# A six-step attention stage with all turns written out, and normalised rows split on ScalarE and GpSimd and transposed by DMA

## What is computed

```python
x = x + 0.5 * ffn(layernorm(x), norm_weight, router_w, router_b, fc1_w, fc1_b, fc2_w, fc2_b)
x = x + attn(layernorm(x), W_q, W_k, W_v, W_o)
x = x + 0.5 * ffn(layernorm(x), ...)

def attn(x, W_q, W_k, W_v, W_o):          # per batch: 512 rows of 256
    q, k, v = x @ W_q.T, x @ W_k.T, x @ W_v.T
    att = softmax(causal(q @ k.T / 16))
    return (att @ v) @ W_o.T

def ffn(x, ...):                          # 8 experts, each takes the 2048 rows of 16384 it rates highest
    xn = x * rsqrt(mean(x * x) + eps) * norm_weight
    probs = softmax(xn @ router_w.T + router_b)
    gates, idx = top_k(probs.T, 2048)
    ye = gelu(xn[idx] @ fc1.T + b1) @ fc2.T + b2
    return scatter_add(idx, ye * gates) / scatter_add(idx, gates)
```

## Time and profile before

| | us |
|---|---|
| median of 3 runs | 2383.83 (2383.52 to 2384.28) |
| profiled execution | 2383.67 |
| its span in the trace | 2382.0 |
| attention stage in the trace, first load to last logits | 977.1 to 1534.3 |

### The profile page before, as it was taken

One profiled execution on the slowest core, in us unless ns is written; L12 is line 12 of the kernel. 1 busy time (PEld: TensorE's weight loads), 2 busy tenths in 40 slices (PEclk: granted clock), 3 DMA queues, 4 the chain that ended last, 5 costly groups with the idle time before them and its releaser, 6 DMA issues.

```text
span 2382.0 us, 44303 instructions
## 1 busy us (share of the span) xinstructions
PE 2006.6 (84%) x15482; PEld 1428.6 (60%) x15482; DVE 1443.8 (61%) x3808; ACT 1402.4 (59%) x2776; POOL 1238.6 (52%) x1527
## 2 busy tenths in 40 slices
PE   4721599999999999499999999511899999999997
PEld 4620266666666667377777777400566666666665
DVE  6988654454454532289888888687644445445431
ACT  6911466666666665266767777401666666666663
POOL 6700566666666663243343443102666676666663
PEclk8655699999999999799999999755999999999998
DMA  8890355564566543232332332200555556456542
GB/s 279 280 312 32 105 103 90 100 118 82 92 116 98 86 74 49 54 99 83 103 105 80 106 99 77 100 1 10 138 95 107 94 100 114 83 94 118 79 68 32
DMA packets 308678, 241.30 MB, mean 101 GB/s; under 512 B 159793, under 2 KB 295985, under 8 KB 308273
## 3 DMA queue, kind: packets, MB, share of 16 engines
q1 hardware_dynamic: 251184, 172.06, 25.9%
q0 software_dynamic: 57344, 67.29, 19.4%
HBM read 120.76 MB, written 101.71 MB: 93 GB/s over the span
## 4 chain that ended last, share of the span: by engine, by line
PE 78%; DVE 12%; ACT 3%; issue 3%; POOL 2%; DMA 2%; SPq 0%; POOLq 0%; DVEq 0%; ACTq 0%
PE ps L1117 24%; PE ps L1119 24%; PE ps L1118 24%; DVE junk L866 5%; PE ps L1138 2%; PE ps L1219 1%; PE ps L1272 1%; ACT zz L612 1%; DVE nmax L1069 1%; DVE bst L793 1%; PE ps L1184 1%; PE ps L1232 1%; DMA z_d<-zz 1%; DVE seen L950 0%; POOL nt L479 0%
## 5 line engine op out<-in xcount | busy, mean ns | idle before, releaser
L978 DVE SCALAR_TENSOR_TENSOR hid_l<-hf,hid_h 128x512 f16<-128x512 f32 x512 | 355.1, 694 | 616.9 <-ACT hid_h L586 603.6
L1117 PE MATMUL ps<-w_h,hid_h 128*128 128x256 f16 x2048 | 558.2, 273 | 0.0
L1118 PE MATMUL ps<-w_l,hid_h 128*128 128x256 f16 x2048 | 558.2, 273 | 0.0
L1119 PE MATMUL ps<-w_h,hid_l 128*128 128x256 f16 x2048 | 558.2, 273 | 0.0
L661 ACT ACTIVATE hf<-ps,b 128x512 f32<-128x512 f32 x512 | 349.0, 682 | 133.2 <-PE ps L1119 121.5
L1117 PE MATMUL ps<-xt,w_h 128*128 128x512 f16 x1024 | 389.7, 381 | 33.9 <-DMA xt<-xs 33.9
L1118 PE MATMUL ps<-xt,w_h 128*128 128x512 f16 x1024 | 389.6, 380 | 0.0
L1119 PE MATMUL ps<-xt,w_l 128*128 128x512 f16 x1024 | 389.6, 380 | 0.0
L586 ACT ACTIVATE hid_h<-hf 128x512 f16<-128x512 f32 x512 | 322.4, 630 | 16.3
L586 ACT ACTIVATE ys<-ps,weight 128x256 f32<-128x256 f32 x256 | 121.5, 474 | 342.7 <-PE ps L1119 342.7
L521 POOL DMA_INDIRECT xe<-z_d,tok x256 | 261.5, 1022 | 100.3 <-issue 77.4
(11 more groups left out here) (225 smaller groups left out, 4016.5 us busy)
## 6 DMA issues: line engine op xcount, KB each, us to landing
w_st<-fc_t SPq DMA_DIRECT2D x32, 1024.0 KB, 5.4
xin<-x SPq DMA_DIRECT2D x32, 512.0 KB, 5.4
z_d<-zz SPq DMA_DIRECT2D x32, 512.0 KB, 4.1
xin<-x_d SPq DMA_DIRECT2D x32, 512.0 KB, 5.3
out<-x SPq DMA_DIRECT2D x32, 512.0 KB, 3.0
z_d<-z SPq DMA_DIRECT2D x32, 512.0 KB, 4.5
xe<-z_d,tok POOLq DMA_INDIRECT x256
xt<-xs SPq DMA_TRANSPOSE x256
```

The source lines that it names most:

```text
L978: dve.scalar_tensor_tensor(hid_l[:, n % 2, f, :], hf[:, f % HF, :], HS, hid_h[:, n % 2, f, :], ALU.mult, ALU.subtract).then_inc(s_hl, 1)
L1117: pe.matmul(dst, lh, rh, start=first, stop=False)
L1118: pe.matmul(dst, lh, rl, start=False, stop=False)
L1119: return pe.matmul(dst, ll, rh, start=False, stop=last)
```

## The change

The attention stage gets one step more. A turn c now does: the load of group c+2; statistics and row factors of group c; the zz rows of z = c-1; u and v of f = c-2; scores to residual of a = c-3; the second normalisation of r = c-4; logits of l = c-5. All 37 turns are written out, without a loop.

The sixteen f32 transposes per turn on TensorE and their PSUM halves zt_h, zt_l, z2t_h, z2t_l are gone. Instead ScalarE copies the normalised rows to f16 (zr, z2r, high half), GpSimd subtracts that from the f32 rows (low half), and SyncE issues four transposing DMAs per group and kind: zr to zc (three buffers) and z2r to z2c (one buffer). u is made in two parts that TensorE's order places apart, and VectorE makes the low half of v at the start of the next turn. xin has eight buffers in this stage, mv, zs and zb four places instead of two.

```diff
+        zr = sb("zr", [P, TG, 2, D], F16, att)
+        zc = sb("zc", [P, 3, 2, KD, S], F16, att)
+        z2r = sb("z2r", [P, TG, 2, D], F16, att)
+        z2c = sb("z2c", [P, 2, KD, S], F16, att)
...
@@ SyncE @@
+            def x_in(c):
+                wait(sp, s_x2, TG * (c - WIDE + 1))
+                sp.dma_start(xin[:, c % WIDE], group(x1_d, c)).then_inc(s_in[c % WIDE], 16)
+            def columns(dst, src, done):
+                for t in range(TG):
+                    sp.dma_start_transpose(dst[:, :, :, t * P:(t + 1) * P].rearrange("p h k s -> p (h k) s"),
+                                           src[:, t].rearrange("p h d -> p (h d)")).then_inc(done, 16)
+            def att_turn(c):
+                z, r = c - 1, c - 4
+                if on(c + 2):
+                    x_in(c + 2)
+                if on(z):
+                    sp.wait_ge(s_zrl, z + 1)
+                    wait(sp, s_s, TG * (z - 2))
+                    columns(zc[:, z % 3], zr, s_zc)
+                if on(r):
+                    sp.wait_ge(s_x2, TG * (r + 1))
+                    sp.dma_start(group(outf, r), x2[:, r % 2]).then_inc(s_x2st[r % 2], 16)
+                    sp.wait_ge(s_z2l, r + 1)
+                    wait(sp, s_lg, NG + r)
+                    columns(z2c, z2r, s_z2c)
+                    sp.dma_start(group(z_d, r), z2[:, r % 2]).then_inc(s_zst[r % 2], 16)
...
@@ GpSimd @@
+            def att_turn(c):
+                z, r = c - 1, c - 4
+                if on(r):
+                    pool.wait_ge(s_mv2, r + 1)
+                    wait(pool, s_z2, r - 1)
+                    row_factors(2 + r % 2, 1).then_inc(s_scale2, 1)
+                if on(z):
+                    pool.wait_ge(s_zrh, z + 1)
+                    pool.tensor_tensor(zr[:, :, 1, :], zz[:, z % 2], zr[:, :, 0, :], ALU.subtract).then_inc(s_zrl, 1)
                 if on(c):
                     pool.wait_ge(s_mv, c + (NG // 2 + 1))
-                    pool.wait_ge(s_z, c + NG)
-                    row_factors(0, 1).then_inc(s_scale, 1)
...
+                    wait(pool, s_z, c + (NG - 1))
+                    row_factors(c % 2, 1).then_inc(s_scale, 1)
+                if on(r):
+                    pool.wait_ge(s_z2h, r + 1)
+                    pool.tensor_tensor(z2r[:, :, 1, :], z2[:, r % 2], z2r[:, :, 0, :], ALU.subtract).then_inc(s_z2l, 1)
+
+            for c in range(NG + DEPTH):
+                att_turn(c)
...
@@ ScalarE, behind the four Exp of group a and pth(a, 0) @@
+                if on(z):
+                    act.wait_ge(s_scale, z + (NG // 2 + 1))
+                    wait(act, s_zrl, z - 1)
+                    rows(zz[:, z % 2], xin[:, z % WIDE], z % 2, (0, 1))
                 if on(a):
                     pth(a, 1)
+                if on(z):
+                    rows(zz[:, z % 2], xin[:, z % WIDE], z % 2, (2, 3)).then_inc(s_z, 1)
                 if on(f):
+                    hi_half(s_u, f, u_h, s_uh, 0)
                 if on(a):
                     pth(a, 2)
+                if on(z):
+                    act.wait_ge(s_z, z + (NG + 1))
+                    wait(act, s_zc, 16 * TG * z)
+                    copy(zr[:, :, 0, :], zz[:, z % 2]).then_inc(s_zrh, 1)
+                if on(a):
                     pth(a, 3)
+                if on(f):
+                    hi_half(s_u, f, u_h, s_uh, 1)
                 if on(r):
...
+                    rows(z2[:, r % 2], x2[:, r % 2], 2 + r % 2, range(TG)).then_inc(s_z2, 1)
+                    act.wait_ge(s_z2, r + 1)
+                    wait(act, s_z2c, 16 * TG * r)
+                    copy(z2r[:, :, 0, :], z2[:, r % 2]).then_inc(s_z2h, 1)
...
@@ VectorE @@
                 if on(a):
                     for q in range(TG):
                         biases(q)
+                    lo_half(s_vh, a, v_flat_l, v_flat_h, s_vl, 0)
+                    lo_half(s_vh, a, v_flat_l, v_flat_h, s_vl, 1)
+                if on(l):
+                    group_logits(l, 7, NG)
                 if on(a):
                     ptl(a, 0)
                     ptl(a, 1)
                 if on(f):
-                    lo_halves(s_th, f + NG, flat(zt_l[:, (u - 1) % 2]), flat(zt_h[:, (u - 1) % 2]), s_tl)
+                    lo_half(s_uh, f, u_l, u_h, s_ul, 0)
...
@@ TensorE @@
+            def u_part(f, m):
+                pe.wait_ge(s_zc, 16 * TG * (f + 1))
+                wait(pe, s_vl, KD * (f - 1) + (m + 1))
...
+            def att_turn(c):
+                f, a, l = c - 2, c - 3, c - 5
                 if on(a):
                     for q in range(TG):
+                        scores(a, a % 3, q)
+                if on(l):
+                    pe.wait_ge(s_ptl, TG * min(a, NG))
+                    pe.wait_ge(s_z2c, 16 * TG * (l + 1))
+                    pe.wait_ge(s_lge, NG + l)
+                    logit_products(7, z2c[:, 0], z2c[:, 1]).then_inc(s_lg, 1)
                 if on(a):
                     pt(a, 0)
                 if on(f):
-                    transposes(ps[2], zz[:, zf], s_tp, rear_read)
+                    u_part(f, 0)
                 if on(a):
                     pt(a, 1)
                     values(a, 0)
                     pt(a, 2)
                     values(a, 1)
                     pt(a, 3)
                 if on(f):
+                    u_part(f, 1)
...
-                    transposes(ps[0], z2[:, (u - 3) % 2], s_z2t, front_read)
                 if on(a):
                     values(a, 2)
                     values(a, 3)
                 if on(f):
+                    v_part(f, 0)
+                    v_part(f, 1)
```

More of the change, by code:

```diff
@@ L306, in on @@
             return not isinstance(g, int) or 0 <= g < NG
-        def turns(engine, turn, steps=None):
-            for c in range(RING):
-                n0 = steps.n if steps else 0
-                turn(c, c)
-            per = steps.n - n0 if steps else 0
-            with engine.Fori(1, NG // RING) as i:
-                for u in range(RING):
-                    if steps:
-                        steps.n = i * (RING * per) + (n0 + (u - RING + 1) * per)
-                    turn(RING * i + u, u)
-            if steps:
-                steps.n = n0 + per * (NG - RING + 1)
-            for c in range(NG, NG + RING):
-                turn(c, c % RING)
+        DEPTH = 5
         def flat(t):
@@ L713, in _, with hi_half @@
             stage_end(act, 2)
-            def hi_halves(ready, n, dst, done, b=4):
-                for k in range(KD):
-                    act.wait_ge(ready, KD * n + (k + 1))
-                    copy(dst[:, k * S:(k + 1) * S], bank(b + k)).then_inc(done, 1)
+            v_flat_h = v_h.rearrange("p (h t) d -> p h (t d)", h=KD)
+            def hi_half(ready, n, dst, done, k):
+                act.wait_ge(ready, KD * n + (k + 1))
+                copy(dst[:, k, :], bank(4 + k)).then_inc(done, 1)
             def pth(a, q):
@@ L724, in pth, with rows @@
                 copy(pt_h[:, q % 2, 0:P * (q + 1)], bank(6 + q % 2)[:, 0:P * (q + 1)]).then_inc(s_pth, 1)
-            def att_turn(c, u):
-                f, a, r = c - 1, c - 2, c - 3
+            def rows(dst, src, at, part):
+                for t in part:
+                    last = act.activation(dst[:, t, :], src[:, t, :], ACT.Identity, bias=zb[:, at, t:t + 1], scale=zs[:, at, t:t + 1])
+                return last
+            def att_turn(c):
+                z, f, a, r = c - 1, c - 2, c - 3, c - 4
                 if on(a):
@@ L1037, in _, with lo_half @@
             stage_end(dve, 2)
-            def lo_halves(ready, n, dst, hi, done, b=4):
-                for k in range(KD):
-                    dve.wait_ge(ready, KD * n + (k + 1))
-                    cols = slice(k * S, (k + 1) * S)
-                    dve.tensor_tensor(dst[:, cols], bank(b + k), hi[:, cols], ALU.subtract).then_inc(done, 1)
+            v_flat_h = v_h.rearrange("p (h t) d -> p h (t d)", h=KD)
+            v_flat_l = v_l.rearrange("p (h t) d -> p h (t d)", h=KD)
+            def lo_half(ready, n, dst, hi, done, k):
+                dve.wait_ge(ready, KD * n + (k + 1))
+                dve.tensor_tensor(dst[:, k, :], bank(4 + k), hi[:, k, :], ALU.subtract).then_inc(done, 1)
             def ptl(a, q):
@@ L1054, in residual @@
                     wait(dve, s_z2, a - 1)
[L1055 removed]
+                    wait(dve, s_x2st[v], 16 * (a // 2))
                     dve.wait_ge(s_prob, TG * (a + 1))
@@ L1097, in att_turn @@
                     residual(a, 3, v, ring)
-                if on(a):
                     dve.wait_ge(s_x2, TG * (a + 1))
-                    wait(dve, s_scale2, a)
-                    stats(x2[:, v], 1).then_inc(s_mv2, 1)
-                if on(f):
-                    lo_halves(s_vh, f, flat(v_l[:, :, :]), flat(v_h[:, :, :]), s_vl)
-            turns(dve, att_turn, steps)
+                    wait(dve, s_scale2, a - 1)
+                    stats(x2[:, v], 2 + a % 2).then_inc(s_mv2, 1)
+            for c in range(NG + DEPTH):
+                att_turn(c)
```

120 lines of the change are left out of this document (36 added, 84 removed).

## The result

The changed kernel takes **2600.4 us** (median of 4 runs, 2599.2 to 2601.4) where the kernel before takes 2384.1 (2383.5 to 2385.3): a ratio of **1.091**, 95% interval 1.089 to 1.093. The forecast was 2616, with a range of 2545 to 2690. Of the kernels further down, e_onedma had one run of 3589 us and b_all one of 6564, for which nothing here gives a reason; their ratios come from the other runs.

A forecast was written before the change was run, and what follows sets the result against it. A loop of handoffs through all five engines was to bound the attention stage: 75 us head, 31 turns of 23.8 (738), less 24, is 789, 232 more than before; 2383.7 + 232 = 2616 us, range 2545 to 2690.

The forecast's parts named there:

- TensorE's work: Attention turn without transposes and pt_l wait: 14.0 us on TensorE, 14.4 with waits, the new turn if nothing else bound.
- steps 1 to 5: Handoffs from TensorE's z2c wait through ScalarE, VectorE, GpSimd, SyncE back to it: 22.1 us, 23.8 with the low clock.
- the other price: GpSimd's z2r subtraction at 4.32 us instead of 2.35, as when VectorE's scan held it; adds 61 us.
- The way through ScalarE: ScalarE's own path to z2r: some 5.5 us after point 2, ending 2 to 3 us before GpSimd is free.
- step 4: GpSimd in program order: row factors 3.92 us ahead of the z2 subtraction 2.35, with 0.08 between, sum 6.35 us.
- the second stream, zc, hides: The zc columns' path has a whole turn more than z2c's and so does not lengthen the loop.
- The clock: TensorE restarts at 1.2 GHz after each gap for at least 2 us, adding 1.7 us to a turn.
- The sentence on the profile to come: TensorE idle some 7 us before the logits, released by DMA z2c<-z2r, turns 23.8 us apart; faster transposes would mean wrong.
- The same loop at full clock: Rival: TensorE's gap is interrupted or its clock returns at once; turn 22.1 us, total 2563 us; 15%.
- a shorter loop: Rival: transposes well under 5.14 us or a step overlapping; turn 18.5 to 21 us, total 2455 to 2545; 7%.
- faster: Rival: TensorE's z2c wait does not bind, its work of 14.4 us is the turn; total 2338 us; 4%.
- one rival: GpSimd's subtraction 4.32 us, or transposes behind the x2 store 1 to 2 us later; 2650 to 2690 us; 17%.

The follow-up runs named there:

- e_onedma: Changed kernel with the four z2c transposes of a group as one DMA of 16 blocks, z2c laid out tile by tile: 2540 us, ratio 1.065.
- b_all: e_step6 with v's residual halves ahead of the row maxima on VectorE and pt_h copies 3 and 4 earlier on ScalarE: 2351.0 us, ratio 0.986.
- e_step6: Changed kernel with the routing logits of a group made one turn later, six turns after its rows come in instead of five: 2381.4 us, ratio 0.998.
- b_both: b_all with the z2c and the zc transposes each as one DMA per group, on other chips: 2418 and 2415 us, ratio 0.980 twice.
- e_sub2: Changed kernel with GpSimd's subtraction for the routing columns (z2r) done twice: 2668.6 us, ratio 1.119.
- e_order: Changed kernel with GpSimd's z2r subtraction ahead of the next group's row factors instead of behind them: 2576.2 us, ratio 1.081.
- e_busy: Changed kernel with 28 dummy matmuls of 512 columns on TensorE ahead of its wait for the routing columns: 2557.3 us, ratio 1.072.

## Why the prediction was right, point by point

The mechanism, the direction and the size hold; 2600.4 lies 15.6 us under the forecast.

- **What bounds the kernel before, and TensorE's work.** Without the transposes TensorE has 14.0 us of work, said the prediction; e_step6 keeps it busy for 14.2 us of a 15.85 us turn, and b_both, whose turn is 14.61, for 96% of the time. Right, nearly to the tenth.
- **The loop, steps 1 to 5.** Predicted 22.1 + 1.7 = 23.8, measured 23.3. Step by step: TensorE with the clock 4.12 and 4.09; ScalarE 1.88 and 1.88; VectorE 4.95 and 4.91; row factors with the gap behind them 4.00 and 3.86; SyncE and landing 6.47 and 6.44. The **mis-sized term is the subtraction on GpSimd**, put at 2.35 from the earlier trace rows and measured at 2.13. The better value stood in the same rows, the 2.14 us that the other one took after VectorE's scan was over. These 0.22 and the 0.14 of the row factors, over 31 turns, are 11 of the 15.6 us.
- **Which GpSimd price.** VectorE was at work on PSUM operands beside it (row maxima at 1320.02 and 1320.88, the subtraction from 1320.34 to 1322.47), and the subtraction took 2.12 to 2.13 us in all 32 groups, never 4.32. This is what the Trainium skill, "SBUF — State Buffer", section "Who interferes with whom", lets pass, and the 2.13 us agree. e_sub2 shows what the other price would have cost: 2.2 us more a turn are 68 us.
- **The way through ScalarE is shorter by 2 to 3 us.** 2.86 measured. That the order of step 4 costs 3.9 us a turn the prediction did not claim, and rightly: e_order gave 1.15 back, since SyncE's zc transposes were a second loop right below. The sentence "the second stream, zc, hides" was true only by that much, and the text had called it merely "a whole turn more".
- **The clock.** Predicted as a fall to 0.50 in the gap with 1.7 us on the loop's TensorE steps; e_busy gives 1.65. "At least 2 us" of low clock after the restart was a cautious reading of the earlier trace rows: it was 6, which changes nothing, since the loop's steps on TensorE are over by then.
- **Head and tail.** The first logits came 72.7 us into the stage (75 predicted), and the last turns saved 22 us (24 predicted).
- **The sentence on the profile to come was wrong in one place.** It said that TensorE's wait would be shown as released by the DMA. It is shown as "issue". Who looks only for the DMA in the list of waits finds nothing and takes a wrong road. It also named transposes issuing faster than 1.29 us as a sign of being wrong; they took 1.27, too small a difference to mean anything.
- **Rivals.** The same loop at full clock is e_busy, 2557 where the rival said 2563. The rule of the Trainium skill, "Advanced Engine Details and Errata", section "X-Bar Transpose (TRN2)", would by the prediction's estimate have made the loop 3.7 us shorter. The runs go against it here: four transposes take 5.12 us of issue for 0.52 MB, and even as one DMA they land in 4.3 us, 122 GB/s. The rival "a shorter loop" has a slip in its sum: 18.5 and 21 us a turn give 2451 and 2529 us in the way of the forecast, not 2455 and 2545. The rival "faster" had the right condition, a wait that doesn't bind, but its price was too good: a turn of 14.4 us needs the waits inside the turn to be 0.4 us, and e_step6, where the wait doesn't bind, has 1.6. It came to 2381, not 2338.

## What to carry to other kernels

When a chain of handoffs is put into a software pipeline, add up the chain from the instruction that waits for its end, along whatever is queued behind that instruction, back to itself. That sum, and not the load of any engine, is the turn, as soon as it is longer than the busiest engine's work; if it is, put the consumer one step later before making any of its stages faster (here 219 us for four changed lines, against 24 to 60 for the best single stage). Waits on all engines at once, the same number of times on each, were the mark of the loop here, and doubling one short operation on an idle engine shows whether it lies on it.

## What the runs showed of the hardware

- A transposing DMA between SBUF buffers, 128 rows of 512 two-byte elements, holds SyncE's queue for 1.27 us (changed kernel, z2c, median of 104; 1.2 to 1.55) and lands 2.5 us after its issue starts. One of 128x2048 holds it for 1.9 us (e_onedma, median of 24; 1.3 to 2.8) and lands after 4.3. So four in one save more than 3 us of queue and 2 us of latency.
- Directly behind the 512 KB store of the rows, four transposes took 5.47 us of issue instead of 5.12 (e_order), not the 1 to 2 us more that one rival allowed; in b_all, with its shorter turns, it was up to 6.05.
- Behind a gap of 6.7 us on TensorE the granted clock was back at 1.00 only after about 6 us of work (changed kernel). With 28 filler products in that gap (e_busy) it left 1.00 once between 1050 and 1650 us, where TensorE stood idle for 1.9 us all the same.
- Matmuls whose 512 moving columns lie in four pieces of 128 in SBUF (b_both) left TensorE's turn at 14.61 us, the same as with one piece.
